# Expert composites from split weights: ScalarE takes the high parts, VectorE the rests

## The chip, the cores and the metric

The kernel runs on one core of a Trainium2 chip. The metric is the device time of one execution in microseconds; the median of several executions counts. The core has five engines that work side by side, each through its own instruction queue in program order: TensorE (PE; its weight loads are PEld), VectorE (DVE), ScalarE (ACT), GpSimd (POOL) and SyncE (SP), which here only issues DMAs. They meet at semaphores.

## What is computed

One block on `x` of 4 x 1024 tokens by 256 features:

```python
xn = layernorm(x)                       # over the features of a token
# attention, 16 heads; out = softmax(Q K^T) V, then normalised over tokens and features
att = norm(attention(xn, Wq, Wk, Wv) + xn)
# experts: 8 of 256 -> 1024 -> 256, two per token with softmaxed gates
logits = xn @ w_gate.T
gates  = softmax over the top 2 of logits, 0 elsewhere
for e in range(8):
    y += gates[:, e] * ((xn @ w_in[e].T) @ w_out[e].T)
return x + att + y
```

An expert has no nonlinearity between its two matrices, so the kernel computes one composite 256 x 256 matrix M_e = w_in[e]^T w_out[e]^T for each expert and applies that to the tokens.

## The kernel before

Three stages follow each other on TensorE.

1. Composites and the first two chunks. The 4096 tokens are 8 chunks of 512. `expert_product(e, s)` (lines 952 to 966) adds half s of expert e's 1024 hidden units to its composite, which lies in two PSUM banks: for each of two 128-wide parts `dh` four products of 128 x 128 by 128 x 256, all in plain fp32. The profile has two records for each of these products. A half is named (e, s), with number i = 2e + s from 0 to 15. Between the halves of experts 1 to 3 stand the transposes (line 921), the value products (`project_v`, 948) and the query and key products (`project_qk`, 932) of chunks 0 and 1; the order is written out by hand in lines 968 to 993, and experts 4 to 7 follow without anything between them.
2. The experts' outputs (`y_bank`, line 1007) for the 32 blocks of 128 tokens, with the projections of the other six chunks between them.
3. Attention (lines 1039, 1061, 1081) over 64 units.

Where a product is not plain fp32 it is a split one: an operand a is stored as a high part, a cast to FP32R, and a rest a - high, and three products (high by high, high by rest, rest by high) stand for one. So it is done for the tokens (`xth`, `xtl`), the projection weights (`wqkh`, `wqkl`, `wvgh`, `wvgl`) and the finished composites: ScalarE casts them out of PSUM (`m_out`, line 486, into `mth`), VectorE subtracts (`m_lo`, line 671, into `mtl`).

Raw weights come through six slots (`win`, `wout`), in `wp` and in the unused halves of `xn` and `acc`. SyncE loads half i (`load_weights`, two DMAs of 512 KB) after TensorE has used half i - 6 in the same slot (`half_done`, `m_ready`, line 283). Its queue holds, in this order: half 0, tokens of chunk 0, the small weights, half 1, then for each expert its two halves, with the tokens of chunks 1 to 3 ahead of experts 1 to 3 and the stores of chunk 0's queries and keys (`qk_out(0)`) behind expert 4.

ScalarE (lines 538 to 559) and VectorE (773 to 804) have their orders written out too: copies and rests of the transposes, the composites and the projections, and on VectorE the token statistics and normalisation of chunks 0 to 3 and the two gate choices of chunks 0 and 1. `kf`, the keys of attention, is set to ones by GpSimd at the start (line 392), as two of its rows stay ones; SyncE's loads into `qf` and `kf` wait for that and for all composites (345, 346).

Of the kernel before, what the change touches and what calls it, by code (L numbers as in the profile page):

```python
# [11 lines left out]
P = 128  # L12
# [3 lines left out]
def attention_and_experts(nc, x, wq_t, wk_t, wv_t, wg_t, w_in, w_out_t, out):  # L16
# [29 lines left out]
    HELD = 4  # L46
    SETS = 3
# [10 lines left out]
    with ctx:  # L58
# [57 lines left out]
        WS = len(win)  # L116
        vb = sb("vb", [P, 2, NKT, VW])
# [55 lines left out]
        half_done = sem("half_done")  # L173
        m_ready = sem("m_ready")
# [98 lines left out]
        def _(sp):  # L273
# [4 lines left out]
            def load_weights(e, s):  # L278

                i = 2 * e + s  # L280
                slot, earlier = i % WS, i - WS
                if earlier >= 0:
                    sp.wait_ge(*((m_ready, KT * (earlier // 2 + 1)) if earlier % 2 else (half_done, earlier // 2 + 1)))
                rows = slice(e * HID + s * HU * P, e * HID + (s + 1) * HU * P)
                for half, w in ((win, w_in), (wout, w_out_t)):
                    sp.dma_start(half[slot], w.rearrange("e h d -> (e h) d")[rows, :]
                                 .rearrange("(p h) d -> p h d", h=HU)).then_inc(w_in_s[slot], 16)
# [94 lines left out]
        def _(pool):  # L382
# [9 lines left out]
            nc.gpsimd.memset(kf[:].bitcast(FP32), 1.0).then_inc(att_const, 1)  # L392

# [6 lines left out]
            for c in range(NC // 2):  # L400
                scale_of_chunk(c)

# [73 lines left out]
        def _(act):  # L476
# [4 lines left out]

            def m_out(e):
# [6 lines left out]
            def xt_out(c):  # L489

                if c >= SETS:
                    act.wait_ge(y_ready[-1], TC * (c - SETS + 1))
                for kt in range(KT):
# [43 lines left out]

            xt_out(0)
            m_out(0)
            for t in range(TC):  # L540
                v_out(0, t)
            for o in range(2):
                qk_copy(0, o)
            m_out(1)
            for o in range(2, 4):
                qk_copy(0, o)
            xt_out(1)
            m_out(2)
            for t in range(TC):
                v_out(1, t)  # L550
            for o in range(2):
                qk_copy(1, o)
            m_out(3)
            for o in range(2, 4):
                qk_copy(1, o)
            m_out(4)
            second_weight(0)
            for e in range(5, E):
                m_out(e)

# [65 lines left out]
        def _(dve):  # L626
# [31 lines left out]
            def xt_lo(c):  # L658
# [3 lines left out]
                for kt in range(KT):  # L662
                    dve.wait_ge(xth_done, KT * c + kt + 1)
                    nc.vector.tensor_tensor(xtl[:, c % SETS, kt, :], ps[:, XT_BANK[kt], :],
                                            xth[:, c % SETS, kt, :].bitcast(FP32), ALU.subtract).then_inc(xtl_done, 1)

# [111 lines left out]
            xt_lo(0)  # L778
            m_lo(0)
            token_statistics(1)  # L780
            normalise_tokens(1)
            for o in range(2):
                qk_lo_half(0, o)
            m_lo(1)
            for o in range(2, 4):
                qk_lo_half(0, o)
            xt_lo(1)
            m_lo(2)
            token_statistics(2)
            normalise_tokens(2)  # L790
            for o in range(2):
                qk_lo_half(1, o)
            m_lo(3)
            for o in range(2, 4):
                qk_lo_half(1, o)
            dve.wait_ge(const_step, 6 + E)
            first_choice(0)
            second_choice(0)
            m_lo(4)
            gate_weights(0)  # L800
            token_statistics(3)
            normalise_tokens(3)
            for e in range(5, E):
                m_lo(e)
# [109 lines left out]
        def _(pe):  # L914
# [37 lines left out]
            def expert_product(e, s):  # L952

                slot = (2 * e + s) % WS
                pe.wait_ge(w_in_s[slot], 32 * ((2 * e + s) // WS + 1))
                for dh in range(KT):
                    if s == 0 and e >= 2:
                        pe.wait_ge(ml_done, KT * (e - 2) + dh + 1)
                    for h in range(HU):
                        last = nc.tensor.matmul(ps[:, M_BANK[e % 2][dh], 0:D], win[slot][:, h, dh * P:(dh + 1) * P],  # L960
                                                wout[slot][:, h, :], start=s == 0 and h == 0,
                                                stop=s == 1 and h == HU - 1)
# [226 lines left out]
```

## Time and profile before

| | us |
|---|---|
| median of 3 runs | 1004.07 |
| lowest, highest | 1003.32, 1004.20 |
| the profiled execution, its time | 1001.28 |
| the profiled execution, its span | 999.5 |
| TensorE busy | 974.0 |
| VectorE busy | 780.2 |
| ScalarE busy | 694.2 |
| GpSimd busy | 285.1 |

The profile is that of one execution. Its page gives the busy time of each engine, a strip of 40 slices, and the chain of work that ended last: followed back from the last instruction to what released each step. The trace behind it can be asked for a stretch: the instructions of an engine in order of time (with the idle time ahead of them in brackets and what ended it), the pieces of the chain, or the busy time in given windows. PEclk is the clock granted to TensorE, 1.00 for 2.4 GHz and 0.50 for 1.2 GHz. A matmul's record lasts longer than its share of the engine, since matmuls overlap; the distance from start to start says what one costs.

### The profile page before, as it was taken

Reading aid. Unit: us, or ns where it says so; the run is one execution under the profiler, and the core shown is the slowest. Engines: PE = TensorE matmul, PEld = TensorE weight load, DVE = VectorE, ACT = ScalarE, POOL = GpSimd, SP = SyncE. Lnnn points to the kernel's source line nnn. Section 1 sums busy time; section 2 is a strip of 40 time slices with the busy share of each in tenths; the row PEclk is TensorE's granted clock in tenths of the full one; section 3 lists DMA queues with packets and bytes.
Section 4 is the critical chain, followed back from the end, with each engine's and each line's share of the span. In section 5 each row is a group of like instructions: output and inputs, shape, how many; then the busy total and the mean of one; then the engine's idle time right before and its main releaser. Section 6 shows DMA issues by size and latency. Waiting matters only on the chain.

```text
span 999.5 us, 20786 instructions
## 1 busy us (share of the span) xinstructions
PE 974.0 (97%) x7816; PEld 504.5 (50%) x7816; DVE 780.2 (78%) x961; ACT 694.2 (69%) x1385; POOL 285.1 (29%) x389
## 2 busy tenths in 40 slices
PE   7999999999998999999999999999999999999994
PEld 6888888888876433333333333333333333333332
DVE  4344454543466899999999999999999999999975
ACT  2312333333322789999989899898989999899994
POOL 2001445544455222223222322223222322223222
PEclk9999999999999999999999999999999999999997
DMA  9967442223200133333333333333333333332204
GB/s 355 366 248 217 144 139 76 72 78 107 88 23 1 43 98 92 97 92 95 92 93 95 88 100 87 97 92 93 94 91 99 86 98 92 95 93 73 73 23 162
DMA packets 127043, 108.59 MB, mean 109 GB/s; under 512 B 81120, under 2 KB 102368, under 8 KB 126944
## 3 DMA queue, kind: packets, MB, share of 16 engines
q1 hardware_dynamic: 122720, 102.81, 35.4%
q10 hardware_dynamic: 4224, 4.46, 1.3%
q8 instruction: 62, 1.02, 0.4%
q14 instruction: 37, 0.30, 0.1%
HBM read 80.75 MB, written 42.21 MB: 123 GB/s over the span
## 4 chain that ended last, share of the span: by engine, by line
PE 96%; POOL 1%; DMA 1%; DVE 1%; issue 1%; ACT 0%; DVEq 0%; SPq 0%; ACTq 0%; POOLq 0%
PE ps L1081 28%; PE ps L1061 22%; PE ps L1007 18%; PE ps L1039 11%; PE ps L960 6%; PE ps L932 4%; PE ps L948 2%; PE ps L1097 1%; PE ps L1109 1%; PE ps L921 1%; DMA wp<-w_out_t 0%; DMA qf<-ot 0%; POOL rden L425 0%; ACT stage L534 0%; DVE xn L885 0%
## 5 line engine op out<-in xcount | busy, mean ns | idle before, releaser
L750 DVE TENSOR_REDUCE negm<-ps 128x1 f32<-128x1024 f32 x512 | 614.8, 1222 | 31.7 <-PE ps L1039 27.3
L585 ACT ACTIVATE wp<-ps 128x512 f32<-128x512 f32 x680 | 368.9, 595 | 43.7 <-PE ps L1061 6.7
L1061 PE MATMUL ps<-qf,kf 50*128 50x512 f32 x1024 | 373.1, 446 | 0.1
L1039 PE MATMUL ps<-kf,qf 48*128 48x512 f32 x1024 | 366.1, 444 | 1.0 <-DVE negm L750 1.0
L1061 PEld LDWEIGHTS ps<-qf,kf 50*128 50x128 f32 x1024 | 152.6, 185 | 199.0 <-ACT wp L585 97.5
L1081 PE MATMUL ps<-wp,vb 128*17 128x256 f32 x2720 | 212.6, 385 | 0.1
L1039 PEld LDWEIGHTS ps<-kf,qf 48*128 48x128 f32 x1024 | 147.2, 185 | 4.3 <-issue 3.9
L425 POOL TENSOR_TENSOR rden<-choice,minus 128x16 f32<-128x16 f32 x31 | 90.3, 2914 | 151.5 <-ACT choice L604 151.5
L585 ACT ACTIVATE picks<-ps 128x512 f32<-128x512 f32 x172 | 102.7, 597 | 22.8 <-PE ps L1061 5.0
L741 DVE SCALAR_TENSOR_TENSOR acc<-ps,gates,acc 128x256 f32<-128x256 f32 x64 | 30.8, 482 | 101.3 <-PE ps L1007 97.2
L1081 PEld LDWEIGHTS ps<-wp,vb 128*17 128x17 f32 x2720 | 46.0, 95 | 122.7 <-ACT vstage L585 53.2
L440 POOL TENSOR_TENSOR mpart<-negm,zero 128x8 fp32r<-128x8 f32 x64 | 12.9, 201 | 321.3 <-DVE negm L750 321.3
L1007 PE MATMUL ps<-mth,xth 128*128 128x512 f32 x256 | 102.6, 401 | 1.2 <-DVE stage L739 0.5
L585 ACT ACTIVATE vstage<-ps 128x512 f32<-128x512 f32 x172 | 101.8, 592 | 1.1 <-PE ps L1061 1.1
L1007 PE MATMUL ps<-mth,xtl 128*128 128x512 f32 x256 | 101.0, 395 | 0.0
L1007 PE MATMUL ps<-mtl,xth 128*128 128x512 f32 x256 | 100.9, 394 | 0.0
L534 ACT ACTIVATE wp<-ps,gates 128x256 f32<-128x256 f32 x96 | 40.3, 471 | 51.1 <-PE ps L1007 51.1
L521 ACT CAST stage<-ps 128x512 fp32r<-128x512 f32 x32 | 18.8, 587 | 60.2 <-PE ps L932 51.2
L1007 PEld LDWEIGHTS ps<-mth,xth 128*128 128x128 f32 x256 | 48.1, 188 | 14.4 <-issue 4.8
L1081 PE MATMUL ps<-picks,vb 128*17 128x256 f32 x688 | 53.9, 385 | 0.9 <-issue 0.8
L408 POOL TENSOR_TENSOR wp<-wp 128x512 f32<-128x512 f32 x24 | 31.1, 1294 | 82.8 <-ACT wp L534 82.8
L1007 PEld LDWEIGHTS ps<-mth,xtl 128*128 128x128 f32 x256 | 48.1, 188 | 11.5
(124 smaller groups left out, 898.9 us busy)
## 6 DMA issues: line engine op xcount, KB each, us to landing
qk_d<-stage SPq DMA_DIRECT2D x64, 256.0 KB
feat_d<-qk_d SPq DMA_DIRECT2D x64, 256.0 KB, 3.3
qf<-feat_d SPq DMA_DIRECT2D x128, 128.0 KB
qf<-feat_d SPq DMA_DIRECT2D x128, 64.0 KB
kf<-feat_d SPq DMA_DIRECT2D x128, 64.0 KB
v_d<-vstage ACTq DMA_DIRECT2D x8, 544.0 KB, 4.8
vb<-v_d SPq DMA_DIRECT2D x128, 34.0 KB, 2.4
acc<-x SPq DMA_DIRECT2D x8, 512.0 KB, 7.2
```

What stands on the lines that cost most here:

```text
L408: nc.gpsimd.tensor_tensor(scaled[:, 0:2], scaled[:, 0:2], scaled[:, 2:4], ALU.add).then_inc(ff_step, 1)
L425: nc.gpsimd.tensor_tensor(rden[:], rows[:, :, :, DH], minus[:], ALU.pow).then_inc(rows_step, 1)
L534: nc.scalar.activation(sums_of(t)[0][:, 2 * (j - BY_VECTOR) + h, :], ps[:, y_bank_of(t, j), h * D:(h + 1) * D], ACT.Copy, scale=gates[:, t ...
L585: nc.scalar.activation(weight_tile(n, j, b)[:, h * HALF:(h + 1) * HALF], ps[:, score_bank(score_turn[unit, b]), :], ACT.Exp).then_inc(exp_ ...
L741: nc.vector.scalar_tensor_tensor(out=total, in0=product, scalar=gate, in1=total, op0=ALU.mult, op1=ALU.add).then_inc(ff_added[j], 1)
L750: nc.vector.tensor_reduce(negm[:, n % 2, qt:qt + 1], ps[:, b:b + 2, :].rearrange("p b c -> p (b c)"), AX.X, ALU.max, negate=True).then_inc ...
L932: last = nc.tensor.matmul(ps[:, PROJECT_BANK[o % 2], :], w[:, o // 2, kt, (o % 2) * P:(o % 2 + 1) * P], v[:, c % SETS, kt, :], start=i == ...
L960: last = nc.tensor.matmul(ps[:, M_BANK[e % 2][dh], 0:D], win[slot][:, h, dh * P:(dh + 1) * P], wout[slot][:, h, :], start=s == 0 and h == ...
L1007: last = nc.tensor.matmul(ps[:, y_bank_of(t, j), :], v[:, t // TC % SETS, kt, tokens], m[:, kt, 2 * j:2 * j + 2, :].rearrange("p e d -> p ...
L1039: last = nc.tensor.matmul(ps[:, MAX_BANK[turn % 2] + half, :], qf[rows, u, qt * P:(qt + 1) * P], kf[rows, u, :], start=True, stop=True)
L1061: nc.tensor.matmul(ps[:, score_bank(score_turn[unit, half]), :], kf[rows, u, j * P:(j + 1) * P], qf[rows, u, h * HALF:(h + 1) * HALF], sta ...
L1081: last = nc.tensor.matmul(ps[32 * c:32 * c + VW, PV_BANK, 0:POS // 4], vb[:, n % 2, j + b * NKT // 2, :], weight_tile(n, j, b)[:, c * (POS ...
```

## The change

The composites of experts 1 to 7 (halves 2 to 15) are made from split weights. For each half ScalarE casts the raw inner and outer weights to FP32R (`high_of_weights`, two casts of 128 x 1024) and VectorE subtracts (`lows_of_weights`, two subtractions of 128 x 1024). GpSimd takes none of the rests. There are two sets of split buffers, used in turn: one in `qf`, one in `kf` and the third buffers of `xth` and `xtl`. A product of a half waits for both rests; a cast of half 4 or later waits until TensorE has used the set, that is for half i - 2. Each fp32 product becomes three split ones. A raw slot is free for the next load once both rests of it are done. As `kf` is in use, its memset moves behind the last composite. On both engines the new calls stand between the old ones, and on VectorE the statistics of chunk 3, its normalisation, the choices and the gate weights are spread among the experts. Expert 0 stays as it was.

```diff
+    WHOLE = 2
+        flat_kf = kf[:].rearrange("p s k -> p (s k)")
+        split = [[qf[:, i, :] for i in range(4)],
+                 [flat_kf[:, 0:POS], flat_kf[:, POS:2 * POS], xth[:, SETS - 1].rearrange("p k t -> p (k t)"),
+                  xtl[:, SETS - 1].rearrange("p k t -> p (k t)")]]
@@ load_weights
-                if earlier >= 0:
-                    sp.wait_ge(*((m_ready, KT * (earlier // 2 + 1)) if earlier % 2 else (half_done, earlier // 2 + 1)))
+                if 0 <= earlier < WHOLE:
+                    sp.wait_ge(*((m_ready, KT) if earlier else (half_done, 1)))
+                elif earlier > 0:
+                    sp.wait_ge(w_in_low, earlier - WHOLE + 1)
+                    sp.wait_ge(w_out_low, earlier - WHOLE + 1)
@@ gpsimd
-            nc.gpsimd.memset(kf[:].bitcast(FP32), 1.0).then_inc(att_const, 1)
...
             for c in range(NC // 2):
                 scale_of_chunk(c)
+            pool.wait_ge(m_ready, KT * E)
+            nc.gpsimd.memset(kf[:].bitcast(FP32), 1.0).then_inc(att_const, 1)
@@ scalar
+            def high_of_weights(i):
+                slot = i % WS
+                act.wait_ge(w_in_s[slot], 32 * (i // WS + 1))
+                if i >= WHOLE + 2:
+                    act.wait_ge(*((m_ready, KT * ((i - 2) // 2 + 1)) if i % 2 else (half_done, (i - 2) // 2 + 1)))
+                nc.scalar.copy(split[i % 2][0], win[slot]).then_inc(w_high, 1)
+                nc.scalar.copy(split[i % 2][2], wout[slot]).then_inc(w_high, 1)
@@ xt_out
+                elif c == SETS - 1:
+                    act.wait_ge(m_ready, KT * E)
@@ scalar, order
             xt_out(0)
+            high_of_weights(2)
             m_out(0)
             for t in range(TC):
                 v_out(0, t)
+            high_of_weights(3)
             for o in range(2):
                 qk_copy(0, o)
+            high_of_weights(4)
             m_out(1)
             for o in range(2, 4):
                 qk_copy(0, o)
+            high_of_weights(5)
             xt_out(1)
+            high_of_weights(6)
             m_out(2)
...
+            high_of_weights(9)
+            high_of_weights(10)
             m_out(4)
-            second_weight(0)
             for e in range(5, E):
+                high_of_weights(2 * e + 1)
+                if e + 1 < E:
+                    high_of_weights(2 * e + 2)
                 m_out(e)
+                if e == E - 2:
+                    second_weight(0)
@@ vector
+            def lows_of_weights(i):
+                for k, raw, low_done in ((0, win[i % WS], w_in_low), (1, wout[i % WS], w_out_low)):
+                    dve.wait_ge(w_high, 2 * (i - WHOLE) + k + 1)
+                    high, low = split[i % 2][2 * k:2 * k + 2]
+                    nc.vector.tensor_tensor(low, raw, high.bitcast(FP32), ALU.subtract).then_inc(low_done, 1)
@@ vector, order
             xt_lo(0)
+            lows_of_weights(2)
             m_lo(0)
             token_statistics(1)
             normalise_tokens(1)
+            lows_of_weights(3)
             for o in range(2):
                 qk_lo_half(0, o)
+            lows_of_weights(4)
             m_lo(1)
...
+            lows_of_weights(9)
             dve.wait_ge(const_step, 6 + E)
+            token_statistics(3)
+            lows_of_weights(10)
+            m_lo(4)
+            normalise_tokens(3)
+            lows_of_weights(11)
             first_choice(0)
+            lows_of_weights(12)
+            m_lo(5)
             second_choice(0)
-            m_lo(4)
+            lows_of_weights(13)
+            lows_of_weights(14)
+            m_lo(6)
+            lows_of_weights(15)
             gate_weights(0)
-            token_statistics(3)
-            normalise_tokens(3)
-            for e in range(5, E):
-                m_lo(e)
+            m_lo(7)
@@ expert_product
-                slot = (2 * e + s) % WS
-                pe.wait_ge(w_in_s[slot], 32 * ((2 * e + s) // WS + 1))
+                i = 2 * e + s
+                if i < WHOLE:
+                    pe.wait_ge(w_in_s[i], 32)
+                    products = [(win[i], wout[i], h) for h in range(HU)]
+                else:
+                    pe.wait_ge(w_in_low, i - WHOLE + 1)
+                    pe.wait_ge(w_out_low, i - WHOLE + 1)
+                    in_high, in_low, out_high, out_low = split[i % 2]
+                    products = [(a, b, h) for h in range(HU) for a, b in ((in_high, out_high), (in_high, out_low), (in_low, out_high))]
...
+                    for k, (a, b, h) in enumerate(products):
+                        last = nc.tensor.matmul(ps[:, M_BANK[e % 2][dh], 0:D], a[:, h, dh * P:(dh + 1) * P], b[:, h, :],
+                                                start=s == 0 and k == 0, stop=s == 1 and k == len(products) - 1)
```

## Rows read from the trace of the kernel before

**Rows 1.** The page: busy time by engine, and the chain that ended last.

```profile
PE 974.0 (97%) x7816; PEld 504.5 (50%) x7816; DVE 780.2 (78%) x961; ACT 694.2 (69%) x1385; POOL 285.1 (29%) x389
...
PE 96%; POOL 1%; DMA 1%; DVE 1%; issue 1%; ACT 0%; DVEq 0%; SPq 0%; ACTq 0%; POOLq 0%
```

**Rows 2.** Windows of the first stage: busy us (instructions) by engine, clock, DMA.

```profile
16.10:55.93 39.83, 39.83 (x210) 34.97 (x208) 17.34 (x47) 12.57 (x35) 2.42 (x4) 1.00 0.96 364
55.93:83.57 27.64, 27.63 (x129) 23.97 (x127) 10.71 (x40) 3.30 (x9) 1.21 (x2) 1.00 0.67 234
```

**Rows 3.** The chain in order of time: start us, us, what, first stage.

```profile
6.09 10.02 PE ps L960 x32
...
16.98 3.46 PE ps L960 x16
...
23.50 2.86 PE ps L932 x12
...
55.93 27.64 PE ps L960 x128
...
85.57 5.59 PE ps L1007 x24
```

**Rows 4.** TensorE in order of time: start us, us, what; chunk 0's value products.

```profile
20.08 0.47 PE L948 MATMUL ps<-wvgh,xth 128*128 128x264 f32 x1
20.39 0.28 PE L948 MATMUL ps<-wvgl,xth 128*128 128x264 f32 x1
...
21.60 0.28 PE L948 MATMUL ps<-wvgh,xtl 128*128 128x264 f32 x1
```

**Rows 5.** ScalarE and VectorE in order of time: splitting the small weights.

```profile
10.28 1.04 ACT L480 CAST wqkh<-stage 128x1024 fp32r<-128x1024 f32 x1
...
12.57 0.71 DVE L776 TENSOR_TENSOR wvgl<-stage,wvgh 128x528 fp32r<-128x528 f32 x1
13.20 1.22 DVE L777 TENSOR_TENSOR wqkl<-stage,wqkh 128x1024 fp32r<-128x1024 f32 x1
```

**Rows 6.** Half 2's outer weights: SyncE's issue, and its DMA to landing (us last).

```profile
7.30 0.43 SPq L286 DMA_DIRECT2D xn<-w_out_t  x1
...
xn<-w_out_t SPq DMA_DIRECT2D x1, 512.0 KB, 9.1
```

**Rows 7.** ScalarE in order of time: the copies of chunk 0's transposes.

```profile
16.58 1.07 ACT L495 CAST xth<-ps 128x512 fp32r<-128x512 f32 x2 [5.26 <-PE ps L921]
```

**Rows 8.** ScalarE in order of time: the last value copy of chunk 0.

```profile
23.60 0.38 ACT L505 COPY vstage<-ps 128x256 f32<-128x256 f32 x1
```

**Rows 9.** VectorE in order of time: choices, statistics, normalisation, rests of a composite.

```profile
57.20 0.21 DVE L696 TENSOR_REDUCE choice<-choice 128x8 f32<-128x64 f32 x1
...
60.01 0.17 DVE L712 TENSOR_TENSOR choice<-choice 128x8 f32<-128x8 f32 x1
...
65.03 1.41 DVE L633 BATCH_NORM_STATS2 st<-acc 128x6 f32<-128x256 f32 x4
...
68.65 1.38 DVE L654 TENSOR_SCALAR xn<-acc,mean,rstd 128x256 f32<-128x256 f32 x4 [1.40 <-POOL rstd L398]
70.07 0.76 DVE L671 TENSOR_TENSOR mtl<-ps,mth 128x256 fp32r<-128x256 f32 x2
```

**Rows 10.** TensorE's gaps (in brackets) and, by windows at the end, its granted clock.

```profile
84.48 1.09 PE L921 MATMUL ps<-ident,xn 128*128 128x128 f32 x8 [0.92 <-DVE mtl L671]
...
984.74 0.66 PE L1097 MATMUL ps<-ident,ot 128*128 128x128 f32 x4 [0.49 <-ACT ot L597]
...
987.00:988.00 1.00, 0.00 (x0) 0.00 (x0) 0.96 (x3) 0.00 (x0) 0.00 (x0) 0.93 1.06 376
988.00:989.00 1.00, 0.00 (x0) 0.00 (x0) 0.28 (x1) 0.00 (x0) 0.64 (x1) 0.50 0.44 155
```

**Rows 11.** GpSimd's memset of kf, and SyncE's first load into qf.

```profile
1.84 1.80 POOL L392 MEMSET kf<- 128x2048 f32 x1
...
94.58 1.51 SPq L325 DMA_DIRECT2D qf<-feat_d  x2
```

More of the change, by code:

```diff
@@ L116, in attention_and_experts @@
         WS = len(win)
+        flat_kf = kf[:].rearrange("p s k -> p (s k)")
+        split = [[qf[:, i, :] for i in range(4)],
+                 [flat_kf[:, 0:POS], flat_kf[:, POS:2 * POS], xth[:, SETS - 1].rearrange("p k t -> p (k t)"),
+                  xtl[:, SETS - 1].rearrange("p k t -> p (k t)")]]
+        split = [[part.rearrange("p (h d) -> p h d", h=HU) for part in parts] for parts in split]
         vb = sb("vb", [P, 2, NKT, VW])
@@ L173, in attention_and_experts @@
         half_done = sem("half_done")
+        w_high = sem("w_high")
+        w_in_low = sem("w_in_low")
+        w_out_low = sem("w_out_low")
         m_ready = sem("m_ready")
@@ L550, in _ @@
                 v_out(1, t)
+            high_of_weights(7)
             for o in range(2):
                 qk_copy(1, o)
+            high_of_weights(8)
             m_out(3)
@@ L786, in _ @@
                 qk_lo_half(0, o)
+            lows_of_weights(5)
             xt_lo(1)
+            lows_of_weights(6)
             m_lo(2)
@@ L790, in _ @@
             normalise_tokens(2)
+            lows_of_weights(7)
             for o in range(2):
                 qk_lo_half(1, o)
+            lows_of_weights(8)
             m_lo(3)
@@ L958, in expert_product @@
                         pe.wait_ge(ml_done, KT * (e - 2) + dh + 1)
[L959 to L962, printed above, removed]
+                    for k, (a, b, h) in enumerate(products):
+                        last = nc.tensor.matmul(ps[:, M_BANK[e % 2][dh], 0:D], a[:, h, dh * P:(dh + 1) * P], b[:, h, :],
+                                                start=s == 0 and k == 0, stop=s == 1 and k == len(products) - 1)
                     if s == 1:
```

## The prediction

> **What bounds the kernel now.** I read the shares of the page first, then the chain of work that ended last, then the same chain in order of time for the first 85 us, where the change lies. TensorE is busy 97% of the span and holds 96% of the chain [rows 1]. So a microsecond that TensorE gains or loses in the first stage goes straight to the end, unless something later waits anyway; the two stages behind (experts' outputs, attention) are touched only by one moved memset. In the first stage TensorE is busy without a gap from the first weights to 83.57 us, VectorE for 17.34 of 39.83 us and then 10.71 of 27.64 us, ScalarE less [rows 2]. That idle time is what the change wants to spend.
>
> **What it gains on TensorE.** A half of an expert is 8 products of 128x256 in fp32; they take 3.46 us, and 128 records in a row take 27.64 us, thus 3.455 us a half [rows 3]. The change makes them 24 products of split operands. This form at 256 columns is not in the trace. The nearest are the split products of 264 columns, 0.121 us apart (ten steps from 20.39 to 21.60) [rows 4], and those of 512 columns, 24 in 5.59 us, 0.233 us apart [rows 3]. The line through the two gives 0.118 us at 256; I take 0.1185. Bounds: 0.108 us (what one of the four passes of an fp32 product takes, 27.64 us / 256) and 0.1225 us, a little over the wider form. A half then takes 24 x 0.1185 = 2.84 us (2.59 to 2.94), 0.61 us less. Fourteen halves change (experts 1 to 7): 8.6 us. Going from an fp32 product to a split one costs about 0.17 us (12 products of 512 columns take 2.86 us here, against 12 x 0.2325 = 2.79 with no such change [rows 3], and behind the first split product after an expert the next starts 0.31 us later, not 0.12 [rows 4]); five such changes become two: 0.5 us. Gain 9.1 us if nothing waits.
>
> **What it adds.** For each of 14 halves: two ScalarE casts of 128x1024 and two VectorE subtractions of 128x1024. The same forms are in the trace on the small weights: 1.04 us and 1.22 us, where the next instruction starts 0.08 us before the end of the last, so 0.95 and 1.14 us each in a row [rows 5]. That is 27 us for ScalarE, with 4 to 5 times as much free, and 32 us for VectorE, which was busy 28 of 67 us: it will be nearly full. Both queues run in program order, so I laid out the five queues in that order, event by event, with these durations (the same layout of the kernel before ends its stage 0.4 us late, at 84.9). For one half the way from its last needed event to TensorE is: cast 1.04, then subtraction 1.14 + 1.22, with hand-overs 3.5 us; and as there are only two sets of split buffers, the cast of half i also waits until TensorE has done half i-2 (0.25 us after its issue).
>
> Stall 1, half (1,0). The raw weights land at 7.30 + 9.1 = 16.4 us [rows 6]. ScalarE copies the transposes first, 16.58 to 17.65 [rows 7]; the casts are then 17.6 to 19.6, VectorE's rests 18.7 to 21.0. TensorE wanted this half at 16.98 [rows 3] and gets it at 21.05: it stands 4.1 us, with everything else queued behind.
> Stall 2, half (1,1). The cast stands behind the last value copy, which in the trace ends 0.5 us after TensorE's last value product [rows 8]. From there: DMA issue 0.4, cast 1.04, rests 2.4, together 4.4 us after the value products; TensorE has 2.8 us of projections to do meanwhile: 1.8 us with hand-overs.
> Stalls 3 and 4, (2,1) and (3,1), come out at 0.5 and 0.1 us in the same way.
> Front, up to the last projection: gain 6 x 0.61 + 0.5 = 4.2, stalls 6.5: 2.3 us lost.
>
> The tail, experts 4 to 7, has nothing on TensorE to cover with, and VectorE carries there: 14 subtractions for halves 9 to 15, 16.0 us; three experts' rests from PSUM, 0.68 us each in a row, 2.0 us; statistics of chunk 3 (1.4 us and six small ones, to 67.25) 2.2 us; normalising 1.4 us; both choices (57.20 to 60.18) 3.0 us [rows 9]. Sum 24.6 us, and 1.7 us of waits ahead of the last half (its cast waits for expert 6's second product). It begins 1.8 us after the last projection (copy and cast) and 2.84 us of products follow: 1.8 + 26.3 + 2.9 = 31.0 us, for what was 27.64 us: 3.2 us lost. In the layout TensorE stands 1.3, 1.6, 1.5, 0.7, 1.6 and 1.2 us ahead of (4,1) to (7,1), with a gain of 8 x 0.61 = 4.9.
> Together: +2.3 + 3.2 = +5.5 us. With a pitch of 0.108 us the layout gives +3.9, with 0.1225 us +6.0.
>
> Edits at nothing: the memset of kf (1.8 us on GpSimd) moves behind the last expert product, where it is done some 8 us before the loads that wait for it come up in SyncE's queue (94.58 us before) [rows 11]; without that cover it would shift these loads by 1.8 us at most, and TensorE uses them only in the stage behind. ScalarE's wait ahead of chunk 2's copies is met already. The raw slots come free by VectorE's rests and no longer by TensorE: loads of halves 9 to 11 go 1.6 us later and the others earlier, while the casts use them 5 us or more after landing. gate_weights goes behind the last rests, but ahead of the first output.
>
> **TensorE's clock.** The stall of 4.1 us has a second price. At the end of the kernel TensorE ends its transposes at 985.4 us and the granted clock goes from 1.00 (2.4 GHz) to 0.50 (1.2 GHz) 2.5 us later (0.93 in the microsecond from 987, so at 987.9); the one gap inside the first stage, 0.92 us, left it at 1.00 [rows 10]. A stall of 4.1 us is longer than 2.5. What a slow stretch costs: the first 32 records of the kernel take 10.02 us instead of 32 x 0.216 = 6.91 [rows 3], so 3.1 us, by the look of it a start at the lower level (the clock column does not show it). I put 0 to 3.1 us on it and take the middle, 1.5 us. The Trainium skill (TensorE: Matmul & The Clock Gate, section "HAM oscillation — how this bites in real kernels") says that a wait for data can cost the fast clock, so that the next group of products starts cold, and the trace of before agrees in its last microseconds. By that rule the stall is paid once as a stall and once again behind it; by the stall alone only once.
>
> **Rivals.**
> A, forecast: the stalls as laid out, and the clock falls once: 5.5 + 1.5 = +7.0 us, 1011.0. Chance 0.50.
> B: the same stalls, clock kept, as after the gap of 0.92 us: +5.5, 1009.5. Against it stands the length of the stall. Chance 0.34.
> C, faster: the side work of VectorE in the tail fits into the gaps and the two sets suffice, so that the tail keeps its whole gain of 4.9 us while the front still loses 2.3: -2.6 us, 1001.5. It decides at the point where a set's way (0.25 + 3.5) and a half's products (2.84) fit into two product times, 5.7 us; by the rows they need 6.6, and VectorE's 24.6 us stand against 7 x 2.84 = 19.9. It holds only if the casts or rests run a fifth faster than on the small weights. Chance 0.05.
> D: half of the stalls is covered by work that the layout puts too late: about +1 us, 1005. Chance 0.06.
> E: the gaps of the tail (35% idle) also lower the clock; each slow half costs up to 2.8 us more, of which the gap takes 1.5: about +16, 1020. No row shows such a mix. Chance 0.05.
> That the split products are no cheaper at all (bound by their weight loads) is excluded by those of 264 columns, which load a 128x128 weight each and stand 0.12 us apart [rows 4].
>
> **How the numbers follow.** The profiled execution has a span of 999.5 us and a time of 1001.28; the median of the runs is 1004.07, 2.8 us above it. I add the difference to each alike: profile about 1008.3 with a span of 1006.5, median 1004.07 + 7.0 = 1011. A's own range is 1009.0 to 1013.0 (pitch -1.6 to +0.5, clock 0 to 3.1), B's 1007.5 to 1010.5. Range 1007.0 to 1013.0: it leaves out C, D, E and little of A. What a measurement here can tell from no change is about 0.2%, 2 us: slower A, B, E: 0.89 less a little of B's lower edge, 0.88; faster C and the edge of D, 0.05; same 0.07.
>
> **What would show it.** In the changed profile: split expert products of 128x256 about 0.12 us apart; TensorE idle about 4 us at 17 to 21 us behind VectorE's first rest, then 1.8 us at about 30 us, and 1 to 1.6 us per half of the tail; the granted clock at 0.50 somewhere in 18 to 25 us (A) or 1.00 throughout (B); VectorE without a gap in the tail; the first output product at 92 to 93 us for 85.6. Wrong: a first stall under 3 us, subtractions well off 1.22 us, or a stage behind that takes back the delay.

## The result, and the profile after

The changed kernel takes 1013.12 us in the median (1012.62 to 1014.51, 4 runs), the kernel before beside it 1003.70 us (1003.22 to 1004.20, 4 runs): ratio 1.0096, 95% interval 1.0079 to 1.0114. It is slower by 9.4 us. The forecast was 7.0 us slower, 1011.0, with a range up to 1013.0: right in sign and kind, too small in size, and the result is just outside the range. The profiled execution took 1013.43 us with a span of 1011.6. The profiled execution of before lies 2.4 us below the median of its runs here, so that the two spans differ by 12.1 us where the medians differ by 9.4.

The page of the changed kernel, busy time by engine and the chain that ended last:

```profile
PE 970.6 (96%) x7928; PEld 504.9 (50%) x7928; DVE 811.6 (80%) x989; ACT 721.3 (71%) x1413; POOL 287.3 (28%) x389
...
PE 90%; DVE 3%; DMA 2%; POOL 1%; ACT 1%; issue 1%; SPq 1%; DVEq 0%; ACTq 0%; POOLq 0%
```

Against [rows 1], TensorE is busy 3.4 us less and the kernel ends later; TensorE's share of the chain fell from 96% to 90%, and VectorE's rose from 1% to 3% of 1011.6 us. That is the whole change in two lines: less to do, and more waiting for it.

Where the time went, TensorE in order of time (start us, busy us, engine, line, operation, shapes, count, in brackets the idle time ahead and what ended it). The 24 products of a half are line 1025:

```profile
16.49 1.04 PE L979 MATMUL ps<-ident,xn 128*128 128x128 f32 x8
...
21.69 4.59 PE L1025 MATMUL ps<-qf 128*128 128x256 f32 x24 [4.16 <-DVE qf L708]
...
33.97 0.36 PE L1025 MATMUL ps<-xth,kf 128*128 128x256 f32 x1 [1.74 <-DVE xtl L708]
...
43.98 0.35 PE L1025 MATMUL ps<-xth,kf 128*128 128x256 f32 x1 [0.38 <-DVE xtl L708]
...
65.75 0.36 PE L1025 MATMUL ps<-xth,kf 128*128 128x256 f32 x1 [1.25 <-DVE xtl L708]
...
70.11 3.11 PE L1025 MATMUL ps<-qf 128*128 128x256 f32 x24 [1.25 <-issue]
...
74.84 0.36 PE L1025 MATMUL ps<-xth,kf 128*128 128x256 f32 x1 [1.61 <-DVE xtl L708]
...
78.35 3.11 PE L1025 MATMUL ps<-qf 128*128 128x256 f32 x24 [0.40 <-issue]
...
82.95 0.36 PE L1025 MATMUL ps<-xth,kf 128*128 128x256 f32 x1 [1.49 <-DVE xtl L708]
...
90.06 0.36 PE L1025 MATMUL ps<-xth,kf 128*128 128x256 f32 x1 [1.12 <-DVE xtl L708]
...
94.08 1.09 PE L979 MATMUL ps<-ident,xn 128*128 128x128 f32 x8 [0.92 <-DVE mtl L714]
```

The first line is the transposes of chunk 0, the last the first transposes behind the last composite, with the same 0.92 us ahead as before [rows 10]. I call the time between these two starts the stage; it leaves out when the first weights land, which differs from run to run by up to 1.7 us. Before it is 84.48 - 15.94 = 68.54 us, after 94.08 - 16.49 = 77.59 us: 9.05 us more, so nearly the whole 9.4 us arises here. Of the 12.1 us between the two spans, 0.55 us are the later first weights, and 2.6 us lie in attention: 1.6 us of them in its first 19 us, where the clock fell for 3.4 us in this execution of after (at 316.1 us) and did not in that of before. Of the fourteen profiled executions, one of each kernel and two of e6's and e9's, seven have a fall there, so it is no sure cost of the change. Nine new waits stand in the stage of after, 13.4 us together.

The granted clock around the first wait, by windows (from:to, length, busy us and instructions of PE, PEld, DVE, ACT, POOL, clock, DMA share, GB/s):

```profile
20.00:22.00 2.00, 0.31 (x3) 0.34 (x3) 2.00 (x4) 0.64 (x3) 0.00 (x0) 1.00 1.04 412
22.60:26.00 3.40, 3.40 (x19) 3.40 (x18) 1.88 (x10) 0.00 (x0) 1.22 (x2) 0.50 1.06 389
26.00:28.00 2.00, 2.00 (x17) 1.91 (x17) 1.13 (x4) 0.66 (x4) 0.00 (x0) 1.00 1.03 400
```

The clock falls to 0.50 (1.2 GHz) 0.9 us after TensorE has begun again, for 3.4 us, and half (1,0) takes 26.11 - 21.69 = 4.42 us for the 2.87 us of an undisturbed half (the next fence): 1.55 us.

The chain in order of time (start us, us, what) shows who made TensorE wait:

```profile
17.13 1.07 ACT xth L518 x2
18.20 0.95 ACT qf L500
...
19.18 2.37 DVE qf L708 x2
...
21.69 4.59 PE ps L1025 x24
...
29.87 0.39 ACTq L532
...
30.31 1.06 ACT kf L500
...
31.46 1.23 DVE kf L708
32.69 1.15 DVE xtl L708
...
33.97 3.11 PE ps L1025 x24
...
50.17 2.87 PE ps L1025 x24
```

The waits shown are each one cast, then two rests, 1.06 + 1.23 + 1.15 us the second time: behind the copies of the transposes (17.13) the first time and behind the issue of the store of the values (29.87) the second. The last line is a half with nothing wrong, 2.87 us; a half behind a wait lasts 2.95 us to the next start (from 33.97 to the projections at 36.92).

### The profile page after: what moved, and what is told of

Same layout as the page of the kernel before. It is cut to its first block, busy times and chain, and to the rows that moved or that the text cites. A ratio compares the mean times of both kernels' runs of the same rounds, so it can differ in the third digit from the quotient of the medians.

```text
span 1011.6 us, 21098 instructions
## 1 busy us (share of the span) xinstructions
PE 970.6 (96%) x7928; PEld 504.9 (50%) x7928; DVE 811.6 (80%) x989; ACT 721.3 (71%) x1413; POOL 287.3 (28%) x389
## 4 chain that ended last, share of the span: by engine, by line
PE 90%; DVE 3%; DMA 2%; POOL 1%; ACT 1%; issue 1%; SPq 1%; DVEq 0%; ACTq 0%; POOLq 0%
PE ps L1145 27%; PE ps L1125 22%; PE ps L1071 18%; PE ps L1103 11%; PE ps L990 4%; PE ps L1025 3%; PE ps L1006 2%; PE ps L1161 1%; PE ps L1173 1%; DMA qf<-ot 1%; DMA wp<-w_out_t 1%; DVE kf L708 1%; DVE xtl L708 1%; PE ps L979 1%; DVE qf L708 0%
```

## The experiments

"Stage" is again the time from the transposes of chunk 0 to those behind the last composite. The kernel before ran beside each: 1002.9 us (9 runs) beside the first four, 1003.01 us (25 runs) beside the next four, 1003.12 us (17 runs) beside e6_again and e9_projection_later, and 1003.23 us (11 runs) beside the last two. As before's own median moves by 0.8 us between these sets, a difference between the medians of two sets is good to about 1 us; the stage is the surer measure. The ratios of e5 and e8 can't be told from 1.

| kernel | stage us | median us (lowest, highest; runs) | ratio to before (95%) |
|---|---|---|---|
| before | 68.54 | 1003.70 (1003.22, 1004.20; 4) | |
| after | 77.59 | 1013.12 (1012.62, 1014.51; 4) | 1.0096 (1.0079, 1.0114) |
| e1_expert1_whole | 72.06 | 1007.62 (1004.53, 1009.61; 6) | 1.0045 (1.0028, 1.0061) |
| e2_fill | 76.11 | 1011.82 (1011.14, 1013.11; 4) | 1.0093 (1.0076, 1.0109) |
| e3_values_first | 73.34 | 1009.17 (1006.97, 1010.57; 4) | 1.0062 (1.0044, 1.0079) |
| e4_no_choices | 76.31 | 1012.47 (1011.23, 1012.92; 4) | 1.0095 (1.0079, 1.0110) |
| e5_high_first | 68.92 | 1003.51 (1001.45, 1005.03; 10) | 0.9997 (0.9977, 1.0016) |
| e8_order_only | 68.62 | 1003.48 (1000.36, 1004.79; 10) | 0.9994 (0.9974, 1.0015) |
| e7_pool_inner | 86.11 | 1020.75 (1020.50, 1021.71; 4) | 1.0168 (1.0125, 1.0211) |
| e6_six_ordered | 63.59 | 1000.18 (997.34, 1006.13; 10) | 0.9972 (0.9949, 0.9996) |
| e6_again | 62.58 | 997.81 (996.80, 998.88; 5) | 0.9948 (0.9936, 0.9960) |
| e9_projection_later | 61.91 | 998.86 (996.90, 1002.63; 12) | 0.9962 (0.9950, 0.9974) |
| e9_again | 61.87 | 998.24 (996.94, 1000.72; 6) | 0.9949 (0.9935, 0.9963) |
| e10_stores_sooner | 61.93 | 996.50 (994.76, 997.69; 6) | 0.9925 (0.9911, 0.9939) |

### Expert 1 left whole

```diff
-    WHOLE = 2
+    WHOLE = 4
@@ scalar order, vector order
-            high_of_weights(2)
-            high_of_weights(3)
-            lows_of_weights(2)
-            lows_of_weights(3)
```

> Expert 1 stays plain fp32 like expert 0 (six experts from split weights; nothing else changes). Theory, that the way of the first split half costs a stall of 4.3 us, a slow stretch of the clock behind it (1.4 us) and a second stall of 1.9 us ahead of half (1,1): all three go, 7.6 us, against 1.2 us of gain given up on two halves, so about 6.4 us less than the changed kernel, near 1006.7 us, and no granted clock of 0.50 before 30 us. Rival, that the sum of VectorE's work bounds the stage: whatever is won in front comes back as stalls in experts 4 to 7, only four subtractions (4.6 us) less, and TensorE idles 3 us more there than in the changed kernel; near 1010.

Measured: the waits ahead of (1,0) and (1,1) are gone, and so is the fall of the clock; one of 0.81 us for a copy of the projections is new. The stage is 5.53 us shorter and the median 5.5 us lower than after's. The waits of the tail are the old ones to 0.2 us (1.07, 1.23, 1.63, 0.39, 1.50, 1.12): nothing is given back later. So the one expert at the front, which could gain 1.2 us, cost 5.5 us net, more than half of the loss.

### The gap filled with products

```diff
             transposes(0)
+            for _ in range(18):
+                nc.tensor.matmul(ps[:, PROJECT_BANK[0], 0:P], ident[:], ident[:], start=True, stop=True)
             expert_product(1, 0)
```

> The changed kernel with 18 products of 128x128 in a free PSUM bank (their results are not used) between chunk 0's transposes and half (1,0), about 3.9 us of work in a stall of 4.3 us. Theory, that the idle stretch lets the clock fall: half (1,0) starts at the same time, takes 2.9 us instead of 4.4, the granted clock stays at 1.00 until the transition to attention, and the kernel is 1.4 to 1.5 us faster, near 1011.7. Rival, that half (1,0) is slow for another reason (its operands, casts that run beside it): it takes 4.4 us again, time unchanged at 1013.

Measured: half (1,0) starts as long after the transposes as in after (5.20 us), the granted clock stays at 1.00 through the stage, and the stage is 1.48 us shorter. The median is 1.3 us lower, but the ratios to before (1.0093 and 1.0096) can't be told apart. All other waits are as after's (1.75, 0.37, then the same six). The 1.48 us is the second price of the 4.2 us wait by itself, against 1.55 us read from the half.

### The values ahead of the first split half

```diff
             transposes(0)
-            expert_product(1, 0)
             for t in range(TC):
                 project_v(0, t)
+            expert_product(1, 0)
```

> On TensorE alone chunk 0's value products go ahead of half (1,0). Theory: they fill part of the wait for the first rests; the idle stretch shrinks to about 1.8 us (wait for the rests of the transposes), the clock stays at 1.00, the stall ahead of half (1,1) falls from 1.9 to 1.3 us; 4.4 us less than the changed kernel, near 1008.7. Rival, VectorE's sum as bound: the front ends earlier but TensorE waits in experts 4 to 7 for the same end of VectorE's rests, at most 1.5 us less.

Measured: stage 73.34, 4.25 us shorter, median 3.95 us lower; the clock stays. The first wait becomes 1.56 us (now for the tokens' rests, ahead of the values), (1,1) waits 1.21 us. The same work in another order takes back nearly half of the loss.

### The choices left out

```diff
-            first_choice(0)
-            second_choice(0)
-            gate_weights(0)
+            nc.vector.memset(gates[:, 0:PAIR * TC], 0.0).then_inc(gates_done, 1)
```

> The two choices and the gate weights of chunks 0 and 1 are left out (their gates are zero, so these tokens miss their experts' part): 4.6 us less work for VectorE in experts 4 to 7. Prediction's reading, that VectorE's sum carries the tail: 4 us less, the last half starts about 86 us into the span instead of 90. Rival, that the two sets of split buffers carry it (a set's turn is cast, rests, products: about 6.9 us an expert): only 1.4 us less, and TensorE stands once per expert, about 1.1 us ahead of its second half, while VectorE has gaps.

Measured: the stage is 1.28 us shorter, as the rival said (1.4), and not 4. TensorE's last two waits in the tail, then the chain between them:

```profile
80.93 0.36 PE L1021 MATMUL ps<-xth,kf 128*128 128x256 f32 x1 [1.03 <-DVE xtl L707]
...
87.94 0.36 PE L1021 MATMUL ps<-xth,kf 128*128 128x256 f32 x1 [1.03 <-DVE xtl L707]
```

```profile
80.93 3.13 PE ps L1021 x24
...
84.34 1.06 ACT kf L500
...
85.43 1.23 DVE kf L707
86.66 1.15 DVE xtl L707
...
87.94 2.16 PE ps L1021 x16
```

For the last two experts the period is 7.01 us and closes on itself: a half's products, then the cast into the set that they leave free, then both rests, then products. No other work of VectorE is in it. In after, the same chain runs on VectorE alone from 71.24 to 82.81 us, through rests and choices. Both limits lie within some 1.3 us of each other over the tail: with 3.4 us of VectorE's busy time away (27.02 and 23.57 us below), the two sets of buffers take over at once. The windows say so too (after, then this run, columns as above):

```profile
61.50:94.00 32.50, 24.54 (x193) 23.28 (x191) 27.02 (x56) 17.24 (x24) 3.75 (x3) 1.00 0.52 184
```

```profile
61.00:92.00 31.00, 23.92 (x191) 22.83 (x189) 23.57 (x37) 16.91 (x23) 3.86 (x3) 1.00 0.50 172
```

VectorE idles 5.5 us of the tail in after, and 7.4 us here.

### The high products first

```diff
-                    pe.wait_ge(w_in_low, i - WHOLE + 1)
-                    pe.wait_ge(w_out_low, i - WHOLE + 1)
-                    products = [(a, b, h) for h in range(HU) for a, b in ((in_high, out_high), (in_high, out_low), (in_low, out_high))]
+                    groups = [([(w_high, 2 * (i - WHOLE) + 2)], [(in_high, out_high, h) for h in range(HU)]),
+                              ([(w_in_low, i - WHOLE + 1)], [(in_low, out_high, h) for h in range(HU)]),
+                              ([(w_out_low, i - WHOLE + 1)], [(in_high, out_low, h) for h in range(HU)])]
```

For each group both parts `dh` are done, then the next group begins, so a rest has a third of the half's time to arrive.

> The changed kernel, but each half's products are sorted: the eight of high by high wait for the two casts alone, the eight with the inner rest for that rest, and the last eight for the outer rest. No instruction is added or left out. Theory, that TensorE waits for the length of a set's way (cast 1.0, rest 1.15, rest 1.2 in a row) and not for VectorE's sum: the wait ahead of half (1,0) falls from 4.3 to 2.8 us, the clock probably stays at 1.00 there, the second wait to 0.5, and the waits in experts 4 to 7 from 7.1 us together to about 4.7; 6.6 us less than the changed kernel if the clock falls all the same and 8.3 if not: 1004.8 to 1006.5. Rival, VectorE's sum as bound: the last rest of half 15 ends when it did, and only its 1.9 us of products that no longer stand behind it are won.

Measured: the work of seven experts is the same, the stage is 68.92 us, 8.67 us shorter than after's and 0.4 longer than before's; the median is 9.6 us below after's, lower than I had expected, but no different from before's. Four small waits are left in the tail, 3.5 us together. The first one of the stage:

```profile
19.39 0.86 PE L1030 MATMUL ps<-qf 128*128 128x256 f32 x5 [2.62 <-ACT qf L501]
```

It is 1.5 us shorter than after's, and the clock stays at 1.00 behind it, which saves the second price of 1.5 us as well.

### The order alone, with expert 1 whole

> As the six experts with the new order, but the products wait for both rests as in the changed kernel. It tells what order and sorting are worth. Theory: about 11.4 us under the changed kernel, near 1001.7, with waits of 0.7 to 1.2 us left in experts 4 to 7 (3.4 us together); the sorted one is 4 us better. Rival: the order brings nothing without the sorting (near 1006.5, as with expert 1 in fp32 alone).

The edit: e1's, and the orders of both engines rewritten as a layout of the queues by measured durations put them. On VectorE, for example, behind S1 X0 N1 S2 (L4 for `lows_of_weights(4)`, M `m_lo`, Q `qk_lo_half`, X `xt_lo`, S and N statistics and normalisation, F and C the choices):

```
Q0.0 Q0.1 L4 N2 M0 Q0.2 Q0.3 L5 X1 M1 L6 S3 L7 F0 M2 Q1.0 Q1.1 L8 Q1.2 C0 L9 M3 L10 L11 M4 Q1.3 L12 L13 M5 L14 L15 N3 M6 M7 G0
```

Measured: stage 68.62, 3.44 us shorter than e1's, with the same instructions. The waits of the tail shrink from 6.9 us together to 3.4 (1.43, 0.80, 0.37, 0.20, 0.33, 0.25), since normalisation and rests of the composites come behind the rests that TensorE is waiting for; the one for a copy of the projections grows from 0.81 to 1.61 us. The median is 4.1 us below e1's, and 1.8 us above the forecast of 1001.7.

### GpSimd takes four inner rests

```diff
+    BY_POOL = (9, 11, 13, 15)
@@ gpsimd
+                pool.wait_ge(w_high, 2 * (i - WHOLE) + 1)
+                nc.gpsimd.tensor_tensor(low, win[i % WS], high.bitcast(FP32), ALU.subtract).then_inc(w_pool_low, 1)
```

> The changed kernel, but GpSimd takes the inner rest of halves 9, 11, 13 and 15, one of 128x1024 at about 2.4 us (1.29 us for 512 and 0.74 us for 256 columns before). VectorE has 4.6 us less in experts 4 to 7, as in the run without choices. Theory: 2.4 us less than the changed kernel, near 1010.7: more than without the choices, since here the way of the odd halves is also shorter (cast 1.05, then 2.4 beside VectorE's 1.2). Rival, that VectorE and GpSimd hinder each other on the same memory: subtractions of VectorE well over 1.22 us beside GpSimd's, and no gain.

Measured: 7.6 us slower than after instead of 2.4 faster; the rival was right. GpSimd and VectorE in order of time:

```profile
63.57 2.37 POOL L421 TENSOR_TENSOR kf<-xn,kf 128x1024 fp32r<-128x1024 f32 x1 [11.51 <-ACT kf L517]
64.47 2.56 DVE L727 TENSOR_TENSOR xtl<-xn,xth 128x1024 fp32r<-128x1024 f32 x1 [1.20 <-ACT xth L518]
...
72.44 3.51 DVE L707 TENSOR_SCALAR xn<-acc,mean,rstd 128x256 f32<-128x256 f32 x4
73.09 2.39 POOL L421 TENSOR_TENSOR kf<-acc,kf 128x1024 fp32r<-128x1024 f32 x1 [0.80 <-ACT kf L517]
...
83.31 2.38 POOL L421 TENSOR_TENSOR kf<-wp,kf 128x1024 fp32r<-128x1024 f32 x1 [7.82 <-ACT kf L517]
83.42 2.35 DVE L760 TENSOR_TENSOR picks<-picks,rank 128x64 f32<-128x64 f32 x1
```

GpSimd's rest ends at 65.94 us; VectorE's, begun at 64.47, ends at 67.03, 1.09 us later, about its own time of 1.22. A tiny operation (0.23 us elsewhere) begun at 83.42 ends at 85.77, just behind GpSimd's end at 85.69. VectorE does not run at half speed beside GpSimd; it stands until GpSimd is done. The Trainium skill (SBUF — State Buffer, section "Who interferes with whom") says that the two share a pair of ports as an exclusive lock, and the trace agrees: 2.56 us for 1.22. So giving GpSimd none of the rests is well chosen in this place. Who comes second stands: in after GpSimd's two small operations for chunk 3's scale, begun beside VectorE's two subtractions (67.66 to 70.01), take 1.12 and 1.86 us; for chunk 2, alone (50.49 us), they take 0.20 and 1.01 us.

```profile
67.82 1.12 POOL L406 TENSOR_TENSOR veps<-var,epst 128x4 f32<-128x4 f32 x1 [16.04 <-DVE var L681]
69.02 1.86 POOL L408 TENSOR_TENSOR rstd<-veps,mhalf 128x4 f32<-128x4 f32 x1
```

In e7 the clock joins in:

```profile
67.17 0.55 PE L1044 MATMUL ps<-xth,kf 128*128 128x256 f32 x1 [2.40 <-DVE xtl L727]
```

```profile
64.70:66.90 2.20, 0.08 (x1) 0.00 (x0) 2.20 (x1) 1.99 (x2) 1.24 (x1) 1.00 0.00 2
66.90:70.30 3.40, 3.13 (x15) 3.16 (x16) 3.29 (x13) 0.19 (x1) 1.06 (x1) 0.50 0.65 240
```

Four waits of 2.3 to 3.0 us in the tail each bring 3.4 us at 1.2 GHz with them; the clock falls inside the first three waits, 0.2 to 0.4 us before their end, and 0.3 us behind the fourth. This is rival E of the prediction, brought about by waits twice as long as after's.

### All three: sorted products, six experts, the new order

> Products sorted as in the last one, expert 1 plain fp32, and the calls on ScalarE and VectorE in another order: casts ahead of the copies of a finished composite, statistics of chunks 2 and 3 and the first choice in VectorE's gaps ahead of expert 4, normalisation of chunk 3 and two projection rests near the end. By the way-of-a-set theory no wait is left on TensorE before the last rests, six experts keep their whole gain of 7 us, and this is the first version below the kernel before: about 15 us under the changed kernel and 6 to 7 under the kernel before, near 996.5. Rival, that products in a row cannot run so densely with both other engines on the same memory, or that the loads come too late for the earlier casts: waits for landings on ScalarE, and 1000 or more.

> The kernel of run e6 once more, beside e9 on one chip, since its ratio to before (0.9972, from 0.9949 to 0.9996) is near the limit of what can be told from no change, and its profiled execution had two stretches at the lower clock behind the first stage. If six experts with sorted products and the new order are truly faster: median 999.5 to 1001, 2 to 3.5 us below before. If that was chance: within 1 us of before.

Measured: no wait for a split half is left at all, in either execution. The stage is 63.59 and 62.58 us, 5.0 and 6.0 us below before's; the medians are 2.8 and 5.3 us below before's beside them, and both intervals lie below 1. The forecast of 996.5 was missed by 3.7 and 1.3 us. The first profiled execution (1006.13 us) had two stretches at the lower clock behind the stage, of 3.4 and 6.8 us, at 137.8 and 465.4 us; the second (997.08 us) had none. The one wait left inside the stage is ahead of chunk 1's third projection: ScalarE may not overwrite `stage` until chunk 0's stores have landed. ScalarE, in the first and in the second execution:

```profile
52.12 1.07 ACT L544 CAST stage<-ps 128x512 fp32r<-128x512 f32 x2 [3.46 <-DMA qk_d<-stage]
```

```profile
49.92 1.07 ACT L544 CAST stage<-ps 128x512 fp32r<-128x512 f32 x2 [2.44 <-DMA qk_d<-stage]
```

### The projections one half later

```diff
             expert_product(3, 1)
+            expert_product(4, 0)
             for o in range(2, 4):
                 project_qk(1, o)
+            expert_product(4, 1)
```

This is TensorE's part; the copies and rests on ScalarE and VectorE are put in that order too.

> Six ordered experts with sorted products (run e6), and the one wait that was left in its first stage taken away: TensorE waited 1.70 us at 53.55 us ahead of chunk 1's third query and key projection, since VectorE's and ScalarE's copies of the first two stood behind the landing of chunk 0's stores at 52.1 us. Here half (4,0), which needs nothing of that, goes ahead of the third and fourth projection, with the copies and rests put in that order too. Theory (the wait was the store's landing, and the place is paid for by nothing else): the wait is at most 0.4 us, the first stage ends at 78 to 79 us (80.54 in e6, 84.48 before), and the median is 1.5 to 2.3 us below e6's, about 998 us, 5 below before. Rival (the wait is given back in the tail, since half (4,1) and its casts then come right behind each other): waits of 1 to 2 us ahead of (4,1) or (5,0), stage end at 80 to 80.5 us, median as e6's, 1000.

> The kernel of run e9 once more, on the same chip as e10, as its median (998.86 us, up to 1002.63) could not be told from e6's. By e9's stage (0.67 us shorter than e6's) less the wait at 135 us that it keeps: 998 to 999 us, ratio to before 0.995 to 0.996.

Measured: the wait inside the stage is gone, and no other has come there, so the rival's mechanism is wrong. But it was only 0.70 us long in e6_again, and the stage is 0.67 us shorter than that one's. The medians, 998.86 and 998.24 us, are not below e6_again's 997.81. Both lie 4 to 5 us below before, although the stage is 6.6 us shorter. Looking for the rest I found a wait of TensorE's in the second stage that neither before nor after has (e9's first execution):

```profile
134.65 0.73 PE L988 MATMUL ps<-xth,wqkh 128*128 128x512 f32 x2 [1.26 <-DVE stage L723]
```

Behind it ScalarE waits for stores again, now those of chunk 2, and SyncE issues these late (ScalarE, then SyncE):

```profile
133.22 1.07 ACT L544 CAST stage<-ps 128x512 fp32r<-128x512 f32 x2 [7.31 <-DMA qk_d<-stage]
```

```profile
109.14 0.89 SPq L337 DMA_DIRECT2D kf<-feat_d  x2
110.08 25.72 SPq L305 DMA_DIRECT2D qk_d<-stage  x11
```

The same wait is 2.47 and 1.39 us in the two executions of e6, and 0.77 us in e9_again. In the two given kernels ScalarE waits for these stores too (before: the first line below; after: 1.23 us, at 143.08), but TensorE does not: the copy comes 51.6 and 49.0 us behind the end of the stage, and 54.6 to 56.3 us behind it in the executions where TensorE waits. A shorter stage is not the only way there: e8, with a stage as long as before's, has a wait of 0.74 us, its copy standing at 138.71 us, 54.6 us behind the stage. Why its stores land 2.6 us later than before's is open. Before, then e8:

```profile
136.07 0.59 ACT L521 CAST stage<-ps 128x512 fp32r<-128x512 f32 x1 [3.78 <-DMA qk_d<-stage]
```

```profile
140.15 0.73 PE L988 MATMUL ps<-xth,wqkh 128*128 128x512 f32 x2 [0.74 <-DVE stage L723]
```

### Chunk 2's stores sooner

```diff
             for n in range(SLOTS):
                 sp.wait_ge(regrouped[n % AHEAD], 16 * (n // AHEAD + 1))
                 features(n)
-            for c in range(PAIR, NC):
+                if n == 1:
+                    qk_out(PAIR)
+            for c in range(PAIR + 1, NC):
                 qk_out(c)
```

> In the kernels whose first stage is 5 to 6.6 us shorter than before's, a wait stands in the second stage that neither before nor after has: TensorE at 134.65 us in e9 (1.26 us), at 135.03 and 138.31 us in the two e6 kernels (1.39 and 2.47 us), for the copies of chunk 3's projections. ScalarE waits there 7.3 us (e9, 133.22) until chunk 2's stores out of stage have landed, and SyncE issues those only from 110.08 us, behind 32 loads of features that attention needs from 300 us on, while the last copy for them is made at 107.3 us. Here the stores of chunk 2 go ahead of the last 16 of these loads; else it is e9. Theory (the time is given back at this place, because SyncE's order was made for a later arrival): ScalarE's wait ends some us sooner, TensorE's wait at 135 us is gone, and the median is 1.0 to 2.0 us below e9's, 997 to 997.8. Rival (the stores land as late as before, since their transfers are what takes long, or the feature loads that now come later make another wait ahead of attention): wait stays, or a new one ahead of 300 us, median as e9's, 998.9.

Measured: ScalarE's first copy for chunk 3 is made at 127.5 us and waits only for TensorE:

```profile
127.50 0.59 ACT L546 CAST stage<-ps 128x512 fp32r<-128x512 f32 x1 [0.59 <-PE ps L990]
```

TensorE's wait at 135 us is gone and none stands elsewhere up to attention. With the same first stage (61.93 us) the median is 996.50 us, 1.74 us below e9's on the same chip and 6.7 us below before's: ratio 0.9925, the whole interval below 1. From the end of the stage to attention it is 221.53 us, against 223.10 and 222.58 in the two executions of e9 and 221.57 before: 1.1 to 1.6 us are won in this place, and the rest of the 1.74 is within what the medians can't tell. This is the fastest of all, some 16 us below the change as it was made.

## Why the prediction was short by a quarter

Set against its steps, in the order of its sum. The stage measures 9.05 us more, the sum said 7.0. The mechanism was right: stalls ahead of the split halves, and a fall of the clock behind the first. What failed is two terms. The gain was put too high, 9.1 us for 8.2, above all by 0.5 us for changes from fp32 to split products that cost nothing; and the stalls were priced by the idle time alone, with nothing for the restart behind each, which cost 0.7 us.

**The gain, 9.1 us forecast, 8.2 measured.** A split half takes 2.87 us, 24 x 0.1195, not 24 x 0.1185 = 2.84: 14 x (3.455 - 2.87) = 8.2 us, 0.4 less. And the 0.5 us for changes from fp32 to split products does not exist. Before, half (1,0) and the value products take 23.50 - 16.98 = 6.52 us [rows 3]; the half by itself is 3.455 and the value products after are 29.20 - 26.11 = 3.09 us: 6.54 together, with nothing left for a change of mode. The 0.31 us that I had read behind the first split product [rows 4] is the first split product's record, which begins 0.18 us early: the fp32 half ahead of it seems to take 3.27 us (16.81 to 20.08) and not 3.455. It cost nothing. The other sign, 2.86 us for 12 products of 512 columns [rows 3], was misread: those stand behind the value products, which are split themselves. Behind an fp32 half, where the change of mode is, such a group takes 2.78 us (the chain of before, half (1,1) and the group behind it):

```profile
26.36 3.45 PE ps L960 x16
29.82 2.78 PE ps L932 x12
```

I read a price from one distance between records and did not close it over the pair of groups.

**The stalls, 14.4 us forecast, 14.8 measured.** One by one, forecast and the idle time shown: (1,0) 4.1, 4.16; (1,1) 1.8, 1.74; (2,1) and (3,1) 0.5 and 0.1, 0.38 and none; the tail 1.3, 1.6, 1.5, 0.7, 1.6, 1.2 against 1.25, 1.25, 1.61, 0.40, 1.49, 1.12. The idle time shown sums to 13.4 us, and from start to start each costs about 0.16 us more: half (4,1) starts 65.75 - 61.48 = 4.27 us after (4,0), 1.40 us over the 2.87 of a half, where the profile shows 1.25. 9 x 0.16 = 1.4. The layout of the queues by durations read from the small weights was good to 0.4 us each.

**The restart, put at nothing, 0.7 us.** A half behind a wait takes 2.95 us, not 2.87, in 8 of the 9 cases (the ninth is the slow one): 8 x 0.08 to 0.09.

**The clock, 1.5 us forecast, 1.55 measured,** and 1.48 by the experiment that keeps TensorE busy. Rival A's condition held in this place, B's did not. That the size fits is luck: 1.5 was the middle of a range from 0 to 3.1. And the 2.5 us of idle time read at the end of the kernel is no measure of when the clock falls: in after it fell 5.1 us after TensorE had gone idle, in e4, at the same wait, 3.9 us after. The Trainium skill's rule (TensorE: Matmul & The Clock Gate, section "HAM oscillation — how this bites in real kernels"), that a wait for data can bring a cold restart, is what the trace shows here.

Together 14.8 + 0.7 + 1.55 - 8.2 = 8.9 of the 9.05 us. The forecast's own terms give 14.4 + 1.5 - 9.1 = 6.8; the 0.2 to 7.0 lie in the tail, where it took 3.2 us lost, between 3.0 by its layout and 31.0 - 27.64 = 3.4 by its sum. The range ended 2.0 us above the forecast. It held the clock and the pitch, but neither the restart nor a doubt about the change of mode, which are 1.2 of the missing 2.1 us. A's own terms, 1011.0 + 0.5 + 1.6, give 1013.1 for its upper end and not 1013.0: whether 1013.12 falls in or out is a matter of a tenth, but the sum was short by 2 us all the same. Between the stage and attention nothing was taken back and nothing added: from the transposes of chunk 0 to the start of attention it is 315.61 - 16.49 = 299.12 us for 306.05 - 15.94 = 290.11 before, 9.01 us more.

**Rivals.** C (the tail keeps its gain) did not happen: from the start of half (4,0), 61.48 us, to 94.08 the tail takes 32.60 us, against 28.71 before (55.77 to 84.48), 3.9 us more. D did not. E did not happen in after, whose waits of at most 1.61 us in the tail left the clock at 1.00, but did in e7 with waits of 2.3 to 3.0 us. "VectorE carries there" is half right: it does from 71 to 83 us, but it idles 5.5 us of the tail and not none, and when it is relieved the two sets hold the tail nearly as long (e4). The sum of VectorE's work gave the right number partly because two limits lie close together.

**Edits at nothing.** The memset of `kf` ran behind the last composite and nothing waited for it; the loads of the raw weights were in time for every cast. Not tried: a third set of split buffers.

## What to carry to other kernels

A cheaper form of a product that needs its operands prepared is paid for in latency: lay out the preparing chain (here cast, rest, rest: 3.5 us) against what TensorE has to do meanwhile, half by half, and leave the form out where there is nothing to cover it; the one expert at the front lost 5.5 us to gain 1.2. If an operand comes in parts, order the products so that each waits for its own part only; that alone took back 8.7 of 9.05 us, with no work saved (1.5 us of it is the clock), and on six experts the order of the side engines' queues took 3.4 us. When a stage or an order changes, look behind it for transfers that now land too late: moving one set of stores forward won 1.1 to 1.6 us there. And close each price that you read from a trace over a group whose total you know, before it goes into a sum.

## What the hardware showed that I had not expected

- The length of a wait does not tell by itself whether the clock falls. It stayed at 1.00 through waits of 2.62 us (e5) and 1.85 us (before, 306 us), and fell with waits of 2.40 us (e7, 66.9 us) and, at the same place of the kernel, 1.87 us (after, 316.1 us); a wait of 4.16 us brought it down in each of the three profiled executions that had it (after, e4, e7).
- VectorE stands behind a long GpSimd operation that reads two operands of SBUF and has begun first: 2.56 us for 1.22, 3.51 for 1.38 [rows 9], 2.35 for 0.23 (e7). GpSimd stands behind VectorE's subtractions in the same way: 1.12 us for 0.20 and 1.86 for 1.01 (after).
- A restart of split products costs 0.08 to 0.09 us beyond the wait, and the idle time that the profile shows ahead of them is 0.16 us less than what is lost.
